# A fused Mamba layer and FFN on one core: where the gate projection lives and when tiles are projected

## The reference

```python
proj = x @ in_proj_w                      # z (2048), xBC (2048 + 512 + 512), dt (32)
xBC  = silu(causal_conv4(xBC) + conv_b)   # -> xs, B, C
h    = dA_t * h + (dt_t * x_t) outer B_t ;  y_t = h @ C_t
y    = y + D * xs
g    = y * silu(z)                        # z is the gate
g    = g * rsqrt(mean(g**2 over a group of 256) + eps) * gate_norm_w
x    = x + residual + g @ out_proj_w
```

## Time and profile before

| | |
|---|---|
| median of 3 runs | 1456.59 us (1456.51 to 1459.61) |
| the profiled execution | 1454.48 us, span 1452.8 us |
| PE busy | 1174.6 us, 81% |
| DVE busy | 1094.2 us, 75% |
| POOL busy | 893.9 us, 62% |
| ACT busy | 778.0 us, 54% |
| mean granted TensorE clock | 0.908 of full speed |

### The profile page before, as it was taken

How to read it: one execution, slowest core, us unless ns; L and a number is a source line. 1 busy time by engine, 2 the same in 40 slices (tenths; PEclk the granted TensorE clock), 3 DMA queues, 4 the chain that set the end, 5 groups by cost and what they waited for, 6 DMA issues and landing times.

```text
span 1452.8 us, 43522 instructions
## 1 busy us (share of the span) xinstructions
PE 1174.6 (81%) x15222; PEld 789.1 (54%) x15222; DVE 1094.2 (75%) x2357; ACT 778.0 (54%) x2058; POOL 893.9 (62%) x848
## 2 busy tenths in 40 slices
PE   2346889898888889887989798979898998886787
PEld 2324565565555555555656555655565565553456
DVE  8735988787678768776878577868787888745895
ACT  2535666555565546554656455656565656531443
POOL 2612577676576657775767576757776777675222
PEclk9975999899899989998999899979999999897999
DMA  5331222222222212222222122222221222111211
GB/s 134 145 88 50 50 71 77 56 60 61 57 71 60 60 54 77 58 65 61 77 60 60 54 74 60 60 69 66 58 70 52 73 64 65 56 34 31 95 32 34
DMA packets 88881, 94.40 MB, mean 65 GB/s; under 512 B 22736, under 2 KB 66384, under 8 KB 88400
## 3 DMA queue, kind: packets, MB, share of 16 engines
q1 hardware_dynamic: 84432, 89.37, 22.0%
q10 hardware_dynamic: 4224, 2.10, 0.5%
HBM read 81.99 MB, written 9.44 MB: 63 GB/s over the span
## 4 chain that ended last, share of the span: by engine, by line
PE 62%; issue 11%; DVE 10%; ACT 8%; POOL 6%; DMA 1%; SPq 1%; ACTq 1%; DVEq 1%; POOLq 0%
PE bank L1339 10%; PE bank L1327 7%; PE bank L1350 7%; PE bank L1454 7%; PE bank L1286 6%; PE bank L1290 6%; PE bank L1443 6%; PE bank L1287 4%; ACT gate L856 2%; ACT xdt L832 2%; PE bank L1408 2%; POOL gated L635 2%; DVE hpk L1068 1%; POOL gated L620 1%; POOL cdec L630 1%
## 5 line engine op out<-in xcount | busy, mean ns | idle before, releaser
L1054 DVE SCALAR_TENSOR_TENSOR conv<-bank,cw,conv 128x511 f32<-128x511 f32 (+2 forms) x576 | 428.0, 743 | 41.5 <-ACT conv L765 39.8
L620 POOL TENSOR_TENSOR gated<-gated,gate 128x512 f32<-128x512 f32 x128 | 163.1, 1274 | 157.4 <-DVE gated L1016 157.4
L641 POOL TENSOR_TENSOR ssum<-ssum,sq 128x512 f32<-128x512 f32 x96 | 123.6, 1288 | 205.6 <-ACT sq L851 205.6
L832 ACT ACTIVATE xdt<-bank,dt_all 128x64 f32<-128x64 f32 x1024 | 223.8, 339 | 20.1 <-DVE xw L1043 20.1
L1068 DVE SCALAR_TENSOR_TENSOR hpk<-hpk,pend,bank 128x64 f32<-128x64 f32 x768 | 211.9, 276 | 12.9 <-DVE hpk L1068 1.0
L1339 PE MATMUL bank<-gated,w_out 128*128 128x512 f32 x256 | 170.5, 754 | 59.1 <-ACT cbs L794 15.7
L856 ACT ACTIVATE gate<-bank 128x512 f32<-128x512 f32 x128 | 76.6, 598 | 241.6 <-PE bank L1290 241.6
L613 POOL TENSOR_TENSOR lm<-lm,cbs 128x512 f32<-128x512 f32 x128 | 163.3, 1275 | 53.9 <-ACT cbs L794 38.2
L765 ACT ACTIVATE conv<-bank,cb_bias,cw 128x512 f32<-128x512 f32 x192 | 149.0, 776 | 69.5 <-PE bank L1290 51.0
L1350 PE MATMUL bank<-ident_t,chan 128*128 128x128 f32 x512 | 128.9, 323 | 65.2 <-ACT gate L856 42.8
L1286 PE MATMUL bank<-xn_hi,w_hi 128*128 (+1 forms) x320 | 162.0, 506 | 23.5 <-ACT xdt L832 23.5
(11 more groups left out here) (175 smaller groups left out, 1749.2 us busy)
## 6 DMA issues: line engine op xcount, KB each, us to landing
spread<-decay_scratch SPq DMA_DIRECT2D x256, 128.0 KB, 3.3
spread<-product_scratch SPq DMA_DIRECT2D x256, 128.0 KB, 3.8
lm<-in_L_attn_in_proj_w SPq DMA_DIRECT2D x1, 2048.0 KB, 8.7
xn_scratch<-chan SPq DMA_DIRECT2D x4, 512.0 KB, 5.1
r_stage<-residual_scratch SPq DMA_DIRECT2D x8, 256.0 KB, 2.7
x_scratch<-r_stage SPq DMA_DIRECT2D x8, 256.0 KB, 3.1
cbs<-x_scratch SPq DMA_DIRECT2D x8, 256.0 KB, 2.8
gated<-x_scratch SPq DMA_DIRECT2D x1, 2048.0 KB, 9.0
```

What stands on the lines that cost most here:

```text
L620: gp.tensor_tensor(gated[:, v % 2, mr, :], gated[:, v % 2, mr, :], gate[:, mr, :], ALU.mult).then_inc(gated_done, 1)
L832: act.activation(xdt[:, r, at:at + HP], xt_bank[:, at:at + HP], ACT.Copy, scale=dt_h).then_inc(xdt_done, 1)
L1054: V.scalar_tensor_tensor(out=conv[:, ci % 4, shift:S], in0=tile_bank(b, n, t)[:, 0:S - shift], scalar=cw[:, q, t, KW - 1 - shift:KW - shif ...
```

## The change

The gate projection leaves `xt_bank` and takes its turn in the two-bank ring: PROJ lists the order of the ten tiles of a unit, and `proj_free` finds what last read the bank (the last tap of a tile, or the silu of a gate). The transposes wait for `xdt` of the slot before. Each slot projects its own first tile, between the first half of the states and the second transposes; `project_next` is gone. The gate projection is last in the slot, save at r = 3, where it stands between `y_intra` and `y_inter`. The variance moves behind `y_intra` and writes its 8 columns in the bank of that slot's gate; `vtok` moves from DVE to ScalarE. On ScalarE the first `chan` silu of the tile before comes ahead of the new tile's start, and the square, then `vtok`, ahead of `xdt`. In slots with one tile, DVE's first tap comes behind state step 0.

```diff
-ORDER = {0: "0123456", 1: "01T23T456T", 2: "0T1T2T3T4T56T"}
+ORDER = {0: "0123456", 1: "0T12T34T56", 2: "0T1T2T3T4T56T"}
+PROJ = [(4 * q + r, t) for q in range(UNITS) for r in range(R) for t in PLAN[r] + ["z"]]
...
-            return proj_bank[CONV_ORDER.index((n // R, t)) % 2]
+            return proj_bank[PROJ.index((n, t)) % 2]
...
+                finish_tile(0)
                 if real:
                     start_tile(PLAN[r][0])
-                if prev is not None:
...
+                finish_tile(1)
...
                     act.activation(dst, gated[:, v % 2, m % R, :], ACT.Square).then_inc(sq_done, 1)
+                if r == 0 and back(b, n, LAG_VAR) is not None:
+                    after(act, var_ready, UNITS, bb, v)
+                    after(act, rstd_done, UNITS, bb, v - 1)
+                    act.activation(vtok[:, :], tile_bank(b, n, "z")[:, 0:2 * CH], ACT.Identity, scale=1.0 / (DI // G),
+                                   bias=eps_c[:, 0:1]).then_inc(var_copied, 1)
+                if ssd is not None:
...
+                            act.activation(xdt[:, r, at:at + HP], xt_bank[:, at:at + HP], ACT.Copy, scale=dt_h).then_inc(xdt_done, 1)
...
-                    act.activation(gate[:, m % R, :], xt_bank[:, :], ACT.Silu).then_inc(gate_done, 1)
+                    act.activation(gate[:, m % R, :], tile_bank(b, n, "z")[:, :], ACT.Silu).then_inc(gate_done, 1)
...
-                    V.tensor_scalar(vtok[:, :], s_bank[:, var_at:var_at + 2 * CH], 1.0 / (DI // G), EPS, ALU.mult, ALU.add).then_inc(var_copied, 1)
...
+                def gate_projection():
+                    bb, m = ssd
+                    if r == 0 and back(b, n, LAG_VAR) is not None:
+                        vb, vm = back(b, n, LAG_VAR)
+                        after(pe, var_copied, UNITS, vb, vm // R)
+                    else:
+                        proj_free(b, PROJ.index((n, "z")))
+                    three_passes(tile_bank(b, n, "z")[:, :], (m // R, CONVS + m % R), bb, z_ready)
...
-                    after(pe, gate_done, SLOTS, bb, m - 1)
+                    xdt_there(pe, bb, m - 1)
                     x_transposes(0)
                 if st is not None:
                     states(0)
+                if real:
+                    project(b, n, PLAN[r][0])
                 if ssd is not None:
                     x_transposes(1)
...
                 small_transposes()
+                two = real and len(PLAN[r]) == 2
+                var = r == 0 and back(b, n, LAG_VAR) is not None
+                if two:
                     project(b, n, PLAN[r][1], y_inputs)
                 else:
                     y_inputs()
+                    if ssd is not None:
                         out_projection()
+                if yy is not None:
+                    y_intra()
+                    intra_finished()
+                if two and ssd is not None:
+                    out_projection()
+                if var:
+                    variance()
+                if ssd is not None and not two and not var:
+                    gate_projection()
+                if yy is not None:
+                    y_inter()
+                if ssd is not None and (two or var):
+                    gate_projection()
-                    three_passes(xt_bank[:, :], (m // R, CONVS + m % R), bb, z_ready)
-                if real and len(PLAN[r]) == 2:
-                    project_next()
```

More of the change, by code:

```diff
@@ L421, in spare @@
             return y_bank[e][:, S // 2:S]
-        var_at = NS * (NBLK - 1)
         def xo_half(b, e):
@@ L1493, in slot @@
-                if r == 0 and back(b, n, LAG_VAR) is not None:
-                    variance()
                 if st is not None:
                     states(1)
-                if real and own_first(b, n):
-                    project(b, n, PLAN[r][0])
                 small_transposes()
-                if real and len(PLAN[r]) == 2:
+                two = real and len(PLAN[r]) == 2
+                var = r == 0 and back(b, n, LAG_VAR) is not None
+                if two:
                     project(b, n, PLAN[r][1], y_inputs)
-                    if yy is not None:
-                        y_intra()
-                    if yy is not None:
-                        intra_finished()
-                    if ssd is not None or st is None:
-                        out_projection()
-                    if yy is not None:
-                        y_inter()
```

117 lines of the change are left out of this document (55 added, 62 removed).

## The result

| | before | after |
|---|---|---|
| median | 1456.55 us (1452.94 to 1459.61) | 1378.34 us (1372.06 to 1385.78, 4 runs) |
| ratio, 95% interval | | 0.9466 [0.9412, 0.952] |
| profiled execution | 1454.48 us, span 1452.8 us | 1385.78 us, span 1384.0 us |
| mean granted clock, that execution | 0.908 | 0.927 |

The change saves 78 us. 22.5 were forecast (1432, range 1416 to 1453): the sign was right, the size was not. First the page of the changed kernel: busy times by engine, and the row of the granted clock in 40 slices.

The account below looks back on a forecast made before the run. TensorE (PE) was taken as the bound, carrying 62% of the chain of waits, with the gate's silu the largest caused wait (42.8 us). 1454.5 - 13.5 (schedule) - 9 (clock) = 1432 us, range 1416 to 1453.

Parts of the forecast that it names:

- +0.10 each: r = 1 and 2: two projections formerly back to back (1.66 us) run apart (0.91 and 0.85), costing +0.10 us per slot.
- the sum: Slot terms give -0.46 us per unit, taken as -0.5 for the second transposes; times 31, with +2, -13.5 us.
- -0.2: r = 0: PE waits about 0.25 us for x times dt behind vtok; slot 9.25 against 9.46 us.
- -0.46: r = 3: gate stall of 0.69 us removed, drain after y_intra adds 0.23; net -0.46 us per slot.
- at no charge: Moves on ScalarE, DVE and POOL priced at nothing, including DVE's first tap behind state 0 and first tile's finish before next start.
- +0.3: Last-but-one slot of a batch: gate projection helps 0.9 us, square, later start and tile cost; +0.3 net, 7 times, +2.
- I take half back: -9: Clock: 12 slow r = 0 output projections cost 18 us; removing stall and variance there returns half, -9 us.
- the first rival: The clock comes back whole: -18 us instead of -9, unit at -0.6, 1420 us; chance 0.20.
- The clock comes back whole: Same schedule, all 18 us of slow r = 0 projections return, unit at -0.6; 1420 us; chance 0.20.
- ScalarE takes it all: ScalarE's longer chain in r = 0, 1, 2 eats the gain: 1454 +- 3 us; chance 0.17 shared with stall only renamed.
- Slower, the clock falls at the end of r = 0: New idles there drop PE's clock in 20 r = 0 slots, 1.5 us each: 1471; 0.15 with longer ScalarE wait.
- The stall only renamed: Transposes wait for x times dt as long as for the gate: 1450 us; chance 0.17 shared with ScalarE takes it all.

Follow-up runs that it names:

- a_tile_front: Changed kernel with each slot's first tile projected ahead of the slot's first transposes, next to the gate projection; 1418.9 us, ratio to before 0.9772.
- a_order_old: Changed kernel with DVE's old order of taps and state steps in one-tile slots; 1371.8 us, ratio to before 0.9457.
- a_start_first: Changed kernel with ScalarE's old order, the new tile's start ahead of the first silu of the tile before; 1407.5 us, ratio to before 0.9708.
- a_control: The changed kernel run again unedited, on the chip of the first experiments; 1377.1 us, ratio to before 0.9489.
- b_control: The changed kernel run again unedited, on a later chip; 1379.8 us, ratio to before 0.95.
- a_stall: Changed kernel with transposes of r = 0 and 1 waiting for the gate's silu again, and r = 3's last gate pass behind y_inter; 1424.2 us, ratio 0.9802.
- a_var_mid2: Changed kernel with r = 0's variance back between second transposes and second state half, and its gate projection ahead of y_inter; 1382.7 us, ratio to before 0.9555.
- a_xdt_first: Changed kernel with ScalarE's old order, x times dt ahead of rexp, square and vtok; 1364.3 us, ratio to before 0.9531.

## Why the prediction was wrong, step by step

**The direction and the mechanism held.** The stall on the gate went, `xdt` took its place with 0.24 us (0.25 forecast), and PE meets ScalarE at the end of r = 0.

**The step that failed in the schedule: "+0.10 each" for r = 1 and 2.** It measured -0.20 and -0.26. I compared a projection alone (0.91) with two back to back, and took the 0.91 from a place between 64-wide matmuls. Between the states and the transposes a tile costs 0.80, and each pair of transposes behind a 512-wide pass costs 0.31 and not 0.36 to 0.46. I named that effect in the sum, at 0.04 per unit; it is some 0.16 in every slot. Against the forecast that is 0.66 per unit, or 20 us over 31 units. It is not what the tile's new place is worth: `a_tile_front`, with two-tile slots of 8.50 (of which 0.2 is its wait for a tap), has the same full-clock time, as the waits of 0.42 and 0.24 go from its one-tile slots, and a unit of it is still 1.1 us shorter than before. What was mis-sized is what the groups cost beside their neighbours.

**r = 0: "-0.2".** It measured -0.35. Variance done at 7.02 (7.17 forecast), hand-over 0.04, `vtok` 0.26, `xdt` 1.75, hand-over 0.04: 9.11. The terms behind the variance held. The 0.15 ahead of them is the output projection's start, 3.97 into the slot for 4.26 (the tile 0.80 for 0.91, the second transposes 0.31 for 0.47), less 0.09 that `y_intra` and its drain took more.

**r = 3: "-0.46".** It measured -0.34. The transposes gained here too, but "at no charge" for DVE's new order was wrong: the last state step comes later and PE waits 0.42 for it. `a_order_old` gives 6.29, which is -0.84.

**"At no charge" for the first tile's silu ahead of the next start.** Against the kernel before, nothing is indeed what it came to: the wait for `rbs` is the same 4.0 us in both. But it is the edit that keeps it so: without it the tile's new place costs 28 us, 9 of them in the schedule (`a_start_first`). I asked only what the silu delays, not what it would be waiting behind.

**n = 14: "+0.3".** The full-clock part is 10.05 against 10.15 (11.04 less half of 1.77), -0.1, and the lower level is gone from it: -0.99 in all. The wait for `xdt` is now in front of the transposes and lasts 1.81 for 2.04.

**The clock: "I take half back: -9".** About 34 came back. Of 18 r = 0 slots (n = 4, 8, 12) 10 had a slow output projection before and none has after: 6.4 us at the lower level per sequence, or 3.2 us of time, 19 over six sequences. In `a_control` none has one either, in `b_control` one of 18. So the 18 of the first rival came back whole. The rest I never priced: per sequence n = 0, 7 and 14 have 2.1, 1.6 and 1.8 us less at the lower level and n = 15 has 3.1 more, which makes 5 us of time at n = 7 and 2 at the ends, and some 7 us came back outside the six sequences. I had counted slow slots only outside the start of a batch, although most of the loss lies around it: 14.2 of 24.5 us at n = 14, 15 and 0.

**The rivals.** *The clock comes back whole* was nearest, 1420, and right for the r = 0 slots; the time went past it since the schedule gave more and the clock came back elsewhere too. *ScalarE takes it all* fell: two-tile slots show no wait on `xdt`. *Slower, the clock falls at the end of r = 0* fell: one of 54 r = 0 slots outside n = 0 fell in three executions. *The stall only renamed* fell too: 42.8 us on the gate became some 9.5 on `xdt` in the ordinary slots. The Trainium skill (TensorE: Matmul & The Clock Gate, "A second HAM failure mode: psum-queue depth-cycling") tells of a bf16 kernel of 512-column matmuls in which frequent small idles between matmul groups make the clock swing. In the r = 0 slot shown above PE idles 0.42, 0.85 and 0.26 us and is granted 1.00 of the clock. Small idles alone do not make it fall here (53 of 54 such slots stayed up), though putting one back (`a_stall`) cost 22 us of clock, and not in the slots where it stands.

**What stays open.** Why the clock falls where it does. Shown is where: at n = 15 and 0, between idles of 1.8 and 3.4 to 4.9 us, at n = 7, behind one of 1.96 (though in two of six sequences each of n = 15 and 7 did not fall), and before in r = 0. Shown too is that six edits of PE's or ScalarE's order each cost 18 to 42 us of clock (the stall, the first tile in front, split or late, the start first, the variance in the middle). But none of them alone brought back the falls in all of n = 4, 8 and 12: `a_stall` has 0.95 us at n = 8, as much as the unedited `b_control`, `a_tile_front` 2.06 at n = 4, `a_var_mid2` none. Which combination held them before was not tried.

## What to carry over

Price a moved group of matmuls by its new neighbours on both sides: the same transposes cost 0.31 or 0.47 us by what stands in front of them. Compare the place of a loss with several executions of one kernel, not with one. When a move removes idle from PE, split each run into full-clock time and clock loss before the forecast, and price the slots that already run slow (here the ends of a sequence) as well as the ordinary ones. "At no charge" needs both questions, what the moved step delays and what it had been queued behind: of the edits entered so, one kept off a loss of 28 us and one was a loss of some 8.

## What was not expected of the hardware

- A pair of 128-column transposes behind a 512-wide pass advances 0.31 us, behind 64-wide matmuls 0.47 (683.57 and 684.50 in `a_tile_front`). Behind a 512-wide pass and even a short wait it advances 0.36 to 0.37 (683.03 in the changed kernel, 706.74 before).
- ScalarE's read of 128x8 from PSUM took 0.27 us (680.98), DVE's of the same block 0.17.
- Behind the same idle of 1.79 to 1.81 us the clock fell in one sequence and not in another of the same execution: n = 15 was granted between 0.62 and 0.99.
- One kernel's clock varies from run to run more than most edits are worth: `a_xdt_first` took 1355.98 to 1389.04 us with a clock loss of 79 to 114. Full-clock time varied by 5 (1271 to 1276).
